# ScalarE instead of GpSimd forms the diagonal blocks for the convolution and the skip term

## The chip, the core and the metric

The kernel runs on one core of a Trainium2 chip. The core has five engines that run side by side and meet at semaphores: TensorE (PE in the rows, its weight loads PEld), VectorE (DVE), ScalarE (ACT), GpSimd (POOL) and SyncE (SP), which only issues DMAs here. The metric is the device time of one execution in microseconds (us), the median of several runs.

## What is computed

A small tower over 32 sequences of 257 tokens with 256 channels: a tokenizer, a layer of four Mamba blocks and a mixture of experts, and a layer of attention and a gated feed-forward part. The change touches only the Mamba blocks, which take the first 9,700 us. Cut to what matters:

```python
def _mamba_block(x, ...):                       # DI = 512 channels, N_ = 16 states, K_ = 4 taps
    xz = _layer_norm(x, g, b) @ in_w
    xs, z = jnp.split(xz, 2, axis=-1)
    xc = conv_general_dilated(xs, conv_w, ..., feature_group_count=DI)   # each channel by itself
    xc = silu(xc + conv_b)
    delta = softplus(xc @ xd_w @ dtp_w + dtp_b)
    dA  = exp(delta[..., None] * A)
    dBx = (delta * xc)[..., None] * Bm[:, :, None, :]
    y = _ssm_scan(dA, dBx, Cm) + D * xc                                  # D * xc is the skip term
    return y * silu(z) @ out_w + res
fwd = blk(blk(x, 0), 1);  bwd = blk(blk(x[:, ::-1], 2), 3)[:, ::-1]
```

## The kernel before

**Jobs.** The sequences are taken two at a time, in 16 groups; a group needs four Mamba blocks, so there are 64 jobs (one block on two sequences), one after the other. A job is of kind 0 to 4: kind 0 is the first of all, then a loop runs 15 times over kinds 1, 2, 3 and 4 (kind 4 is the first block of the next group), and the last group has kinds 1, 2 and 3 alone. That makes 1, 16, 16, 16 and 15 jobs of kinds 0 to 4. A last phase of some 1,700 us does everything behind the Mamba layer, and the change does not touch it.

**States and units.** Channels lie on the 128 partitions, in four chunks c. A job walks through 64 states s = 16 c + n. For each state ScalarE writes the decays exp(delta A) (`decays`, L714), GpSimd writes B times u (`b_times_u`, L489, called bu below), VectorE scans the two sequences with two instructions (`scan`, L912) and multiplies by C (`c_times_h`, L928), for every fourth state (s = 1, 5, 9, ...) GpSimd does that product (L498), and TensorE adds the product to y by four transposes (`add_state`, L1159). Two states make a unit u = s // 2, so a job has units 0 to 31. Ordinary decays are kept for two states ahead only, in PSUM; six of a job go to a buffer in SBUF (early_decay, states 22 to 24 and 50 to 52, or two to six states later in kinds 2 and 4), so that ScalarE can run a silu with its two table loads meanwhile. bu is kept for four states.

**Work between the states.** Each engine has its own hand-written list of what it does in which unit; the lists meet only at semaphores, and each engine takes its instructions strictly in order. Between the scans of a job the next one is prepared: norm (ScalarE `centred` L586 and L589, `inverse_deviation` L596 and L599, VectorE `normalize` L882), input product, convolution, silu, projections, and the softplus for delta. Of that softplus VectorE does two SCALAR_TENSOR_TENSOR instructions for each chunk (`step_size`, L891 and L896) and GpSimd the last sum (L469) and the product u (L475). For chunks 0 and 1 of the next job VectorE's pair stands in units 29 and 30 of kinds 0, 1 and 3, and in units 30 and 31 of kinds 2 and 4. Once a job VectorE forms the product cb of two SBUF tensors (`first_gains`, L939, unit 9), and three times it takes a finished chunk of y from TensorE (`output`, L948).

**The diagonal blocks.** TensorE does the convolution as four products with diagonal matrices, one for each tap, and the skip term as one. GpSimd forms them from the identity: `conv_weights` writes four blocks of 128x128 for a chunk into diag_store (L448, and three times L450), `skip_weights` one into skip_diag (L460). A job has 16 + 4 = 20 such instructions, 1,280 in all. On GpSimd they stand at states 21 and 25 (chunks 0 and 1), 38 and 40 (chunks 2 and 3; 40 and 42 in kinds 2 and 4), and at states 12, 28, 44 and 60 (skip), each behind the bu of that state. GpSimd's bu of a state waits only for the scan four states earlier, so GpSimd works ahead, until its own product with C (L498) has to wait for the scan of that state.

```python
if s % NST == 12 and not (last and s > 3 * NST):
    skip_weights(g, jj, s // NST + 1)
if s in (21, 25):
    conv_weights(g, jj + 1, (s - 21) // 4)
if s in (2 * conv_at(jj) + 10, 2 * conv_at(jj) + 12):
    conv_weights(g, jj + 1, 2 + (s - 2 * conv_at(jj) - 10) // 2)
```

## Time and profile before

| | us |
|---|---|
| median of 3 runs | 11426.39 (11422.36 to 11435.52) |
| the profiled execution | 11426.99 |
| its span, from first to last instruction | 11425.2 |
| first scan of the first job | 120.8 |
| last scan of the last job | 9702.5 |
| a job of kind 1, 2, 3, 4 (window from first scan to first scan, one job each) | 140.7, 148.6, 155.2, 156.4 |
| busy: VectorE, TensorE, GpSimd, ScalarE | 8852.6, 8675.4, 7499.2, 5872.3 |

A row of the timeline gives the start in us from the span's start, the time, engine, line, operation, what is written and read, and in brackets how long the engine had been idle and what ended that. A repeated row has a count (x3) and the time from the start of the first to the end of the last. The jobs repeat each other closely: the two-input instructions of VectorE in units 29 to 31 start within 0.02 us of the same place in all jobs of a kind, and the one that takes 1.51 us in the rows of kind 1 below takes 1.50 or 1.51 us in all 32 jobs of kinds 0, 1 and 3.

### The profile page before, as it was taken

Reading aid. Unit: us, or ns where it says so; the run is one execution under the profiler, and the core shown is the slowest. Engines: PE = TensorE matmul, PEld = TensorE weight load, DVE = VectorE, ACT = ScalarE, POOL = GpSimd, SP = SyncE. Lnnn points to the kernel's source line nnn. Section 1 sums busy time; section 2 is a strip of 40 time slices with the busy share of each in tenths; the row PEclk is TensorE's granted clock in tenths of the full one; section 3 lists DMA queues with packets and bytes.
Section 4 is the critical chain, followed back from the end, with each engine's and each line's share of the span. In section 5 each row is a group of like instructions: output and inputs, shape, how many; then the busy total and the mean of one; then the engine's idle time right before and its main releaser. Section 6 shows DMA issues by size and latency. Waiting matters only on the chain. (4 is left out here: it accounts for less than half of the span.)

```text
span 11425.2 us, 153089 instructions
## 1 busy us (share of the span) xinstructions
PE 8675.4 (76%) x42776; PEld 6977.0 (61%) x42776; DVE 8852.6 (77%) x13553; ACT 5872.3 (51%) x8819; POOL 7499.2 (66%) x7270
## 2 busy tenths in 40 slices
PE   6777776777777777777777777777777776799998
PEld 5656565655656565656555656565565665577776
DVE  5888888888888888888888888888888889233332
ACT  4555555555555555555555555555555554244443
POOL 5877777777777777777777878777777777000000
PEclk8888887888888888888888888888888887899999
DMA  2212122222222122222222212222222211000000
GB/s 81 80 65 70 64 80 75 80 70 77 74 75 73 63 70 75 80 75 80 70 78 75 73 52 80 75 80 75 75 74 73 80 67 46 25 10 10 11 11 10
DMA packets 366103, 730.02 MB, mean 64 GB/s; under 512 B 143670, under 2 KB 188890, under 8 KB 365274
## 3 DMA queue, kind: packets, MB, share of 16 engines
q1 hardware_dynamic: 361560, 717.54, 18.4%
q8 instruction: 341, 5.59, 0.2%
q14 instruction: 488, 4.00, 0.1%
q10 hardware_dynamic: 3714, 2.89, 0.1%
HBM read 699.27 MB, written 21.05 MB: 63 GB/s over the span
## 5 line engine op out<-in xcount | busy, mean ns | idle before, releaser
L489 POOL TENSOR_TENSOR bu<-b_all,u_buf 128x514 f32<-128x514 f32 x4096 | 4943.6, 1231 | 427.0 <-DVE h_ps L912 362.3
L912 DVE TENSOR_TENSOR_SCAN h_ps<-decay,bu 128x256 f32<-128x256 f32 x5468 | 3727.1, 738 | 498.9 <-ACT decay L714 298.4
L714 ACT ACTIVATE decay<-delta,neg_a 128x512 f32<-128x512 f32 x3712 | 2541.8, 688 | 3045.8 <-DVE h_ps L912 2041.7
L1159 PE MATMUL y_ps<-ident,ch 128*128 128x128 f32 x16384 | 2693.5, 313 | 901.5 <-DVE ch L928 460.2
L1159 PEld LDWEIGHTS y_ps<-ident,ch 128*128 128x128 f32 x16384 | 2216.4, 162 | 1419.3 <-DVE ch L928 673.5
L498 POOL TENSOR_TENSOR ch<-ch,c_all 128x512 f32<-128x512 f32 x1024 | 1427.8, 1394 | 1596.5 <-DVE ch L912 1596.1
L928 DVE TENSOR_TENSOR ch<-h_ps,c_all 128x512 f32<-128x512 f32 x3072 | 1979.2, 672 | 0.0
L912 DVE TENSOR_TENSOR_SCAN ch<-decay,bu 128x256 f32<-128x256 f32 x1956 | 1439.4, 736 | 40.7 <-ACT decay L714 36.4
L1044 PE MATMUL w_ps<-xn,in_w 128*128 128x257 f32 x4096 | 1111.8, 417 | 221.1 <-ACT xn L605 160.1
L1044 PEld LDWEIGHTS w_ps<-xn,in_w 128*128 128x128 f32 x4096 | 806.6, 209 | 408.1 <-issue 166.2
L1044 PE MATMUL w_ps<-xs_pad,diag_store 128*128 128x257 f32 x4096 | 983.1, 386 | 12.4 <-ACT xc L632 12.4
L1507 POOL TENSOR_TENSOR rstd_F<-h_F 128x514 f32<-128x514 f32 x16 | 17.5, 1096 | 1434.0 <-DMA h_F<-h_mid 1434.0
L1044 PEld LDWEIGHTS w_ps<-xs_pad,diag_store 128*128 128x128 f32 x4096 | 754.6, 193 | 118.4 <-ACT xc L632 25.4
L912 DVE TENSOR_TENSOR_SCAN h_ps<-early_decay,bu 128x256 f32<-128x256 f32 x676 | 774.3, 1201 | 48.6 <-DVE sz L948 42.6
L1044 PE MATMUL w_ps<-sz,out_w 128*128 128x257 f32 x2048 | 527.9, 403 | 292.2 <-DVE cen L871 180.8
L948 DVE TENSOR_TENSOR sz<-w_ps,sz 128x512 f32<-128x512 f32 x256 | 176.5, 689 | 618.0 <-PE w_ps L1171 618.0
L1044 PEld LDWEIGHTS w_ps<-sz,out_w 128*128 128x128 f32 x2048 | 391.0, 199 | 362.2 <-DVE cen L871 186.8
L1152 PE MATMUL y_ps<-skip_diag,xc 128*128 128x128 f32 x2048 | 362.1, 334 | 251.2 <-ACT y_t L691 251.2
L1152 PEld LDWEIGHTS y_ps<-skip_diag,xc 128*128 128x128 f32 x2048 | 339.7, 244 | 280.1 <-ACT y_t L691 259.7
L1044 PE MATMUL w_ps<-dtbc,dt_w 32*128 32x257 f32 x1024 | 433.0, 545 | 64.6 <-ACT rstd L658 62.1
L1044 PE MATMUL w_ps<-xc,xp_w 128*64 128x257 f32 x1024 | 301.6, 459 | 131.8 <-ACT xc L638 131.8
L1171 PE MATMUL w_ps<-ident,y_t 128*128 128x128 f32 x1024 | 187.1, 314 | 259.1 <-ACT y_t L691 259.1
(250 smaller groups left out, 11519.9 us busy)
## 6 DMA issues: line engine op xcount, KB each, us to landing
b_all<-bc_dram SPq DMA_DIRECT2D x512, 514.0 KB, 4.8
c_all<-bc_dram SPq DMA_DIRECT2D x512, 514.0 KB, 6.3
in_w<-in_L_attn_in_w SPq DMA_DIRECT2D x64, 1024.0 KB, 5.0
x_in<-in_x SPq DMA_DIRECT2D x128, 256.0 KB, 2.6
out_w<-in_L_attn_out_w SPq DMA_DIRECT2D x64, 512.0 KB, 3.9
...
```

The costliest lines, as they stand in the source:

```text
L489: pool.tensor_tensor(bu[:, s % NBU, :, :].rearrange("p b s -> p (b s)"), b_all[:, n // NU, n % NU, :, :].rearrange("p b s -> p (b s)"), u_ ...
L498: pool.tensor_tensor(h, h, c_all[:, n // NU, n % NU, :, 1:], ALU.mult).then_inc(pool_c_done, 1)
L714: func(decay_slot(jj, s).rearrange("p (b t) -> p b t", b=NB), delta[:, c, :, 1:S], ACT.Exp, scale=neg_a[:, k, c, n:n + 1]).then_inc(decays ...
L912: last = dve.tensor_tensor_scan(h[:, cols], decay_slot(jj, s)[:, cols], bu[:, s % NBU, b, 1:], bu[:, s % NBU, b, 0:1], ALU.mult, ALU.add)
L928: dve.tensor_tensor(ch[:, s % NPR, :].rearrange("p (b t) -> p b t", b=NB), h_ps[:, s % NU, :].rearrange("p (b t) -> p b t", b=NB), c_all[: ...
L948: dve.tensor_tensor(sz[:, c, :, 1:], banks(f"y{c}", g, jj).rearrange("p (b t) -> p b t", b=NB), sz[:, c, :, 1:], ALU.mult).then_inc(read_o ...
L1044: last = pe.matmul(w[0:rows, b, 0:S], lhs, rhs, start=(i == 0), stop=(i == len(terms(b)) - 1))
L1152: pe.matmul(y_ps[:, k, :], xc[:, jj % 2, c, b, 1 + half * P:1 + (half + 1) * P], skip_diag[:, :], start=(k == 0), stop=False, skip_group_c ...
L1159: last = pe.matmul(y_ps[:, k, :], ch[:, s % NPR, k * P:(k + 1) * P], ident[:, :], is_transpose=True, start=False, stop=(n == NST - 1 and k ...
L1171: last = pe.matmul(w[:, k * P:(k + 1) * P], y_t[:, k, :], ident[:, :], is_transpose=True, start=True, stop=True, skip_group_check=True)
L1507: pool.tensor_tensor(rstd[s][:, :, :], h[s][:, 0, :, :], h[s][:, 1, :, :], ALU.add).then_inc(h_summed[s], 1)
```

## The change

Both helpers move from GpSimd's list to ScalarE's. An ACTIVATE with the function Identity and the diagonal's weights as its scale takes the place of each GpSimd instruction, one for one. They wait for the same events as before. On ScalarE `conv_weights` stands in units 10 and 12 (chunks 0 and 1) and in the units conv_at + 5 and conv_at + 6 (chunks 2 and 3; these are units 19 and 20, or 20 and 21 in kinds 2 and 4), and `skip_weights` in units 5, 13, 21 and 29, each behind the unit's second ordinary decay. For the first job they stand in the preparation itself.

```diff
--- before.py
+++ after.py
@@ -433,33 +433,6 @@
             pool.affine_select(out=ident[:, :], in_=ident[:, :], compare_op=ALU.not_equal, fill=1.0, base=0,
                                pattern=[[-1, P]], channel_multiplier=1).then_inc(ident_set, 1)
 
-            def conv_weights(g, jj, c):
-
-                k = BLOCK_OF_JOB[jj % 4]
-                if c < 2:
-                    if positive(job_count(g, jj - 1, CI, CI)):
-
-                        pool.wait_ge(delta_ready, job_count(g, jj - 1, CI, CI))
-                else:
-                    pool.wait_ge(full_of(f"cv{c - 2}", g, jj), nth(f"cv{c - 2}", g, jj))
-                for tap in range(KW):
-                    weight = conv_w[:, k, c, tap:tap + 1]
-                    if tap == 0:
-                        last = pool.tensor_tensor(conv_diag[:, c % 2, tap, :], ident[:, :], weight.to_broadcast([P, P]), ALU.mult)
-                    else:
-                        last = pool.tensor_scalar(conv_diag[:, c % 2, tap, :], ident[:, :], weight, 1.0, ALU.mult, ALU.mult)
-                last.then_inc(diag_ready, 1)
-
-            def skip_weights(g, jj, c):
-
-                jj, c = jj + c // CI, c % CI
-                k = BLOCK_OF_JOB[jj % 4]
-                if positive(job_count(g, jj, STATES, NST * (c - 1) + 1)):
-
-                    pool.wait_ge(y_added, job_count(g, jj, STATES, NST * (c - 1) + 1))
-                pool.tensor_tensor(skip_diag[:, :], ident[:, :], d_skip[:, k, c:c + 1].to_broadcast([P, P]), ALU.mult
-                                   ).then_inc(skip_diag_ready, 1)
-
             def step_size(g, jj, c):
 
                 pool.wait_ge(sp_sums, job_count(g, jj, 2 * CI, 2 * c + 2))
@@ -518,9 +491,6 @@
             def lead_in():
                 pool.wait_ge(consts_loaded, 16 * n_const_dmas)
                 pool.wait_ge(ident_set, 2)
-                for c in range(CI):
-                    conv_weights(0, 0, c)
-                skip_weights(0, 0, 0)
                 step_size(0, 0, 0)
                 delta_x(0, 0, 0)
                 step_size(0, 0, 1)
@@ -536,16 +506,10 @@
                         step_size(g, jj, (s - 3) // 2)
                     if s % NST == 11 and s < 3 * NST:
                         delta_x(g, jj, s // NST + 1)
-                    if s % NST == 12 and not (last and s > 3 * NST):
-                        skip_weights(g, jj, s // NST + 1)
                     if s == 3 * NST + 6:
                         first_tokens(g, jj)
                     if last:
                         continue
-                    if s in (21, 25):
-                        conv_weights(g, jj + 1, (s - 21) // 4)
-                    if s in (2 * conv_at(jj) + 10, 2 * conv_at(jj) + 12):
-                        conv_weights(g, jj + 1, 2 + (s - 2 * conv_at(jj) - 10) // 2)
                     if s == STATES - 1:
                         step_size(g, jj + 1, 0)
                         delta_x(g, jj + 1, 0)
@@ -555,6 +519,29 @@
         @block.scalar
         def _(act):
             func = nc.scalar.activation
+
+            def conv_weights(g, jj, c):
+
+                k = BLOCK_OF_JOB[jj % 4]
+                if c < 2:
+                    if positive(job_count(g, jj - 1, CI, CI)):
+
+                        act.wait_ge(delta_ready, job_count(g, jj - 1, CI, CI))
+                else:
+                    act.wait_ge(full_of(f"cv{c - 2}", g, jj), nth(f"cv{c - 2}", g, jj))
+                for tap in range(KW):
+                    weight = conv_w[:, k, c, tap:tap + 1]
+                    last = func(conv_diag[:, c % 2, tap, :], ident[:, :], ACT.Identity, scale=weight)
+                last.then_inc(diag_ready, 1)
+
+            def skip_weights(g, jj, c):
+
+                jj, c = jj + c // CI, c % CI
+                k = BLOCK_OF_JOB[jj % 4]
+                if positive(job_count(g, jj, STATES, NST * (c - 1) + 1)):
+
+                    act.wait_ge(y_added, job_count(g, jj, STATES, NST * (c - 1) + 1))
+                func(skip_diag[:, :], ident[:, :], ACT.Identity, scale=d_skip[:, k, c:c + 1]).then_inc(skip_diag_ready, 1)
 
             def tokens(g, jj, c):
 
@@ -740,6 +727,7 @@
                 softplus_start(0, 0, 2)
                 softplus_powers(0, 0, 2)
                 act.wait_ge(setup_act, 7)
+                skip_weights(0, 0, 0)
                 for s in range(NDP):
                     decays(0, 0, s)
 
@@ -751,6 +739,8 @@
 
             def prepare_back(g, jj):
                 for c in (0, 2):
+                    conv_weights(g, jj, c)
+                    conv_weights(g, jj, c + 1)
                     conv_input(g, jj, c)
                     conv_input(g, jj, c + 1)
                     conv_output(g, jj, c)
@@ -847,6 +837,12 @@
                     lead(g, jj, NU * u + NDP, last)
                     after_even(g, jj, u, first, last)
                     lead(g, jj, NU * u + NDP + 1, last)
+                    if u % PAIRS == 5 and not (last and u > 3 * PAIRS):
+                        skip_weights(g, jj, u // PAIRS + 1)
+                    if not last and u in (10, 12):
+                        conv_weights(g, jj + 1, (u - 10) // 2)
+                    if not last and u in (conv_at(jj) + 5, conv_at(jj) + 6):
+                        conv_weights(g, jj + 1, u - conv_at(jj) - 3)
                     if u in silu_at(jj):
                         for i in range(NDS):
                             decays(g, jj, NU * u + NDP + 2 + i)
```

GpSimd, from the product with C of state 57 to that of state 61, in every job with a next one (before, then after; REGISTER_ALU computes a count to wait for):

```order
L498 TENSOR_TENSOR ch<-ch,c_all 128x512
L488 REGISTER_ALU
L489 TENSOR_TENSOR bu<-b_all,u_buf 128x514
L460 TENSOR_TENSOR skip_diag<-ident,d_skip 128x128
L489 TENSOR_TENSOR bu<-b_all,u_buf 128x514
L488 REGISTER_ALU
L489 TENSOR_TENSOR bu<-b_all,u_buf 128x514
L488 REGISTER_ALU
L489 TENSOR_TENSOR bu<-b_all,u_buf 128x514
L496 REGISTER_ALU
L498 TENSOR_TENSOR ch<-ch,c_all 128x512
```

```order
L471 TENSOR_TENSOR ch<-ch,c_all 128x512
L461 REGISTER_ALU
L462 TENSOR_TENSOR bu<-b_all,u_buf 128x514 x2
L461 REGISTER_ALU
L462 TENSOR_TENSOR bu<-b_all,u_buf 128x514
L461 REGISTER_ALU
L462 TENSOR_TENSOR bu<-b_all,u_buf 128x514
L469 REGISTER_ALU
L471 TENSOR_TENSOR ch<-ch,c_all 128x512
```

The skip block between the bu of state 60 and that of state 61 is gone, so the four bu follow each other directly.

ScalarE, units 12 and 13 of kind 4, around the silu of the gates (before, then after; sz is the gate, cen and sq belong to the norm of the next job):

```order
L714 ACTIVATE decay<-delta,neg_a 128x512
L714 ACTIVATE early_decay<-delta,neg_a 128x512 x3
L681 ACT_TABLE_LOAD
L681 ACTIVATE sz<-sz 128x2056
L682 ACT_TABLE_LOAD
L586 ACTIVATE sq<-w_ps 128x514
L589 ACTIVATE cen<-w_ps 128x514
```

```order
L701 ACTIVATE decay<-delta,neg_a 128x512
L534 ACTIVATE diag_store<-ident,conv_w 128x128 x4
L701 ACTIVATE early_decay<-delta,neg_a 128x512 x3
L668 ACT_TABLE_LOAD
L668 ACTIVATE sz<-sz 128x2056
L669 ACT_TABLE_LOAD
L544 ACTIVATE skip_diag<-ident,d_skip 128x128
L573 ACTIVATE sq<-w_ps 128x514
L576 ACTIVATE cen<-w_ps 128x514
```

Four blocks of the convolution now stand ahead of the three early decays and the silu, and one skip block between the silu and the norm. In the other kinds the silu of the gates stands in unit 9, ahead of all blocks of its surroundings.

## Rows read from the trace of the kernel before

**Rows 1.** Profile page: busy us by engine, then groups (count, busy, mean ns, idle)
```profile
PE 8675.4 (76%) x42776; PEld 6977.0 (61%) x42776; DVE 8852.6 (77%) x13553; ACT 5872.3 (51%) x8819; POOL 7499.2 (66%) x7270
...
L912 DVE TENSOR_TENSOR_SCAN h_ps<-decay,bu 128x256 f32<-128x256 f32 x5468 | 3727.1, 738 | 498.9 <-ACT decay L714 298.4
...
L948 DVE TENSOR_TENSOR sz<-w_ps,sz 128x512 f32<-128x512 f32 x256 | 176.5, 689 | 618.0 <-PE w_ps L1171 618.0
```

**Rows 2.** Groups of GpSimd by form, the same columns: the blocks
```profile
L450 POOL TENSOR_SCALAR diag_store<-ident,conv_w 128x128 f32<-128x128 f32 x768 | 273.0, 373 | 0.0
...
L448 POOL TENSOR_TENSOR diag_store<-ident,conv_w 128x128 f32<-128x128 f32 x256 | 121.4, 474 | 80.8 <-PE w_ps L1044 61.1 <-DMA ln_b<-in_L_attn_ln_b 19.7
L460 POOL TENSOR_TENSOR skip_diag<-ident,d_skip 128x128 f32<-128x128 f32 x256 | 102.3, 400 | 0.0
```

**Rows 3.** Timeline of ScalarE, start of the run: four of the new kind
```profile
24.96 1.26 ACT L728 ACTIVATE tok_ident<-ident,tok_wb 128x128 f32<-128x128 f32 x4
```

**Rows 4.** Timeline, GpSimd and VectorE, kind 1, unit 2
```profile
3287.90 1.26 POOL L469 TENSOR_TENSOR delta<-sp_l,rstd 128x514 f32<-128x514 f32 x1
...
3288.03 1.69 DVE L891 SCALAR_TENSOR_TENSOR sq<-sq 128x514 f32<-128x514 f32 x1
```

**Rows 5.** Timeline, GpSimd then VectorE, kind 2, units 29 and 30
```profile
3550.28 1.10 POOL L489 TENSOR_TENSOR bu<-b_all,u_buf 128x514 f32<-128x514 f32 x1
3551.33 0.41 POOL L460 TENSOR_TENSOR skip_diag<-ident,d_skip 128x128 f32<-128x128 f32 x1
...
3551.69 1.29 POOL L489 TENSOR_TENSOR bu<-b_all,u_buf 128x514 f32<-128x514 f32 x1
...
3552.93 1.10 POOL L489 TENSOR_TENSOR bu<-b_all,u_buf 128x514 f32<-128x514 f32 x1
...
3553.94 0.68 DVE L891 SCALAR_TENSOR_TENSOR diag_store<-diag_store 128x514 f32<-128x514 f32 x1
```

**Rows 6.** Timeline, GpSimd then VectorE, kind 1, units 29 and 30
```profile
3402.01 1.27 POOL L489 TENSOR_TENSOR bu<-b_all,u_buf 128x514 f32<-128x514 f32 x1
...
3404.76 1.26 POOL L489 TENSOR_TENSOR bu<-b_all,u_buf 128x514 f32<-128x514 f32 x1
...
3403.15 0.69 DVE L896 SCALAR_TENSOR_TENSOR sp_l<-sp_l,diag_store 128x514 f32<-128x514 f32 x1
...
3405.06 1.51 DVE L891 SCALAR_TENSOR_TENSOR sq<-sq 128x514 f32<-128x514 f32 x1
```

**Rows 7.** Timeline, ScalarE then VectorE, kind 1, units 10 to 13
```profile
3323.63 0.59 ACT L589 ACTIVATE cen<-w_ps 128x514 f32<-128x514 f32 x1
3326.73 0.69 ACT L596 ACTIVATE rstd<-w_ps,eps_t 128x514 f32<-128x514 f32 x1 [2.51 <-PE w_ps L1044]
...
3335.01 0.69 ACT L714 ACTIVATE decay<-delta,neg_a 128x512 f32<-128x512 f32 x1 [1.81 <-DVE h_ps L912]
...
3328.13 0.69 DVE L948 TENSOR_TENSOR sz<-w_ps,sz 128x512 f32<-128x512 f32 x1 [3.57 <-PE w_ps L1171]
```

**Rows 8.** Timeline of VectorE, kind 1, unit 9: cb
```profile
3314.09 0.41 DVE L939 TENSOR_TENSOR cb<-b_all,c_all 128x32 f32<-128x32 f32 x1
```

**Rows 9.** Timeline, ScalarE, TensorE, GpSimd, VectorE, kind 4, units 12 to 15
```profile
3774.90 1.94 ACT L714 ACTIVATE early_decay<-delta,neg_a 128x512 f32<-128x512 f32 x3
...
3788.56 0.60 PE L1171 MATMUL w_ps<-ident,y_t 128*128 128x128 f32 x4
...
3778.16 0.39 POOL L460 TENSOR_TENSOR skip_diag<-ident,d_skip 128x128 f32<-128x128 f32 x1
3778.52 3.55 POOL L489 TENSOR_TENSOR bu<-b_all,u_buf 128x514 f32<-128x514 f32 x3
...
3778.39 4.24 DVE L912 TENSOR_TENSOR_SCAN h_ps<-early_decay,bu 128x256 f32<-128x256 f32 x1 [0.40 <-POOL bu L489]
...
3789.79 0.68 DVE L948 TENSOR_TENSOR sz<-w_ps,sz 128x512 f32<-128x512 f32 x1
3790.69 2.20 DVE L882 TENSOR_TENSOR cen<-cen,rstd 128x514 f32<-128x514 f32 x2 [0.23 <-DVE sz L948]
```

## The prediction

> **What bounds the kernel now.** I read the page first, then the timeline of single jobs, unit by unit. VectorE is the busiest engine of the whole run, 8852.6 us, with TensorE close behind (8675.4); GpSimd has 7499.2 and ScalarE 5872.3 [rows 1]. All of VectorE's Mamba work lies ahead of 9702.5 us, and there it is the bound: its scans have only 498.9 us of idle time before them in 5468 instructions, and the largest single wait is that for a chunk of y from TensorE, 618.0 us before L948 [rows 1]. So I ask of each edit one question: does it move an instruction of VectorE, or something that VectorE waits for? Seconds taken from GpSimd are worth nothing in themselves.
>
> **What is removed.** GpSimd loses 768 instructions of 373 ns, 256 of 474 ns and 256 of 400 ns: 273.0 + 121.4 + 102.3 = 496.7 us [rows 2], 7.8 us a job. GpSimd works up to four states ahead and then waits for VectorE's scan at its own product with C, once in four states, so this time mostly becomes longer waiting there. Its direct worth is nil where a later bu still comes before its scan, which is everywhere but at two kinds of places costed below: where the change moves the moments at which the two engines meet in SBUF, and the stall of unit 12 of kind 4.
>
> **What is added.** ScalarE gets 1,280 instructions. The trace has none with a diagonal weight, but four of the same function, size and operand sort, 1.26 us for four in a row [rows 3], 0.31 us each: 1280 × 0.315 = 403 us, ScalarE's busy time from 5872 to some 6275 us (a shorter one, if the first of the four carries a fixed start, would give 370). It remains the least busy. What counts is whether a decay comes late. In kind 1 ScalarE idles 2.51 us before L596 in unit 10, where a block of four (1.26) goes in, and 1.81 us before the decay of unit 12, where the second goes in [rows 7]. The blocks for chunks 2 and 3 (units 19 to 21) and the single skip instruction of 0.31 us stand where decays are two states ahead of VectorE, that is more than one scan pair (2 × 0.7 us). I take 0 for kinds 0 to 3; the bounds are 0 and 0.3 us a job (one skip instruction exposed), 0 and +15 us in all. The added ACTIVATEs are Identity and change no table: no table load is added. The lead-in pays the skip instruction ahead of the first decays, +0.3 us once, and the conv blocks stand beside loads.
>
> **What moves: where VectorE and GpSimd meet.** This is the term I think decides. In the trace a VectorE instruction with two SBUF inputs that arrives while a GpSimd instruction is running does not take its usual time. L891 began at 3288.03, while L469 of GpSimd ran from 3287.90 to 3289.16: it took 1.69 us [rows 4]. Undisturbed it takes 0.68 [rows 5]. The rest of L469 was 1.13, so the price is the rest plus 0.56. A second case: bu63 of kind 1 ran from 3404.76 to 3406.02, L891 began at 3405.06 and took 1.51 = 0.96 + 0.55 [rows 6]. So I use: time = rest of the GpSimd instruction + 0.55 us, against 0.66 to 0.69 with none running. The skip block between bu60 and bu61 takes 0.36 to 0.41 us; without it bu61, bu62 and bu63 come 0.36 us earlier, because nothing else holds them, while VectorE's instructions of units 29 and 30 stay where they are.
>
> Kinds 2 and 4 (31 jobs). Now bu60 starts at 3550.28 and the skip block at 3551.33; bu61 (1.29) and bu62 (1.10, from 3552.93 to 3554.03) follow, and L891 starts at 3553.94, in the gap between bu62 and bu63, and takes 0.68 [rows 5]. After: bu61 at 3551.33, bu62 at 3552.57, bu63 at 3553.61 to 3554.88 (1.27, as the bu63 of [rows 6] has it at 1.26). L891 arrives at 3553.94 with 0.94 of bu63 still to go: 0.94 + 0.55 = 1.49 instead of 0.68, **+0.81 us**. A scan follows it on VectorE and nothing there has been waiting for another engine, so it is passed on: 31 × 0.81 = +25.1 us. Bounds: 0, if VectorE wins the meeting as it does now, and 1.29 − 0.16 (a bu63 that starts just before L891) or 1.1 us: 0 to +34.
>
> Kinds 0, 1 and 3 (32 jobs). Now L896 at 3403.15 takes 0.69 beside nothing (bu61 of 3402.01 ends at 3403.28, 0.13 later), and L891 at 3405.06 takes 1.51 [rows 6]. After: bu61 runs from 3401.65, bu62 (1.10, as in [rows 5]) from 3402.88 to 3403.98, so L896 takes 0.83 + 0.55 = 1.38, +0.69. bu63 then follows at 3404.4 at the latest (behind L896, or from 3403.94 on if it goes first) and ends by 3405.65, while L891 has moved to 3405.75 (3405.06 + 0.69): nothing runs, 0.66 instead of 1.51, −0.85. Together **−0.16 us**, 32 × −0.16 = −5.1 us. The nearest miss: if bu63 ended 0.1 us later, L891 would be caught by its tail (0.1 + 0.55 = 0.65), which costs the same. Bounds: −0.85 (L896 not caught) and +0.69 (L891 still caught): −27 to +22 us.
>
> The skip blocks of states 12, 28 and 44 move bu in the same way, but only one instruction of VectorE with two SBUF inputs is near: cb at 3314.09, 0.41 us, in unit 9 of kinds 1 to 3 [rows 8], which bu22 would now meet after the skip block of state 12 is gone from ahead of it: up to 0.7 us. Two units later VectorE waits 3.57 us for y from TensorE [rows 7], whose chain does not pass through cb. That cover hides it; without it 48 × 0.7 = 34 us would be due.
>
> **Kind 4, units 12 to 15** (15 jobs) is the one place where ScalarE's additions are not covered. There the block of four stands ahead of the three early decays at 3774.90 [rows 9], and the skip instruction behind the silu ahead of the norm: 1.26 + 0.31 = 1.57 us on the chain early decays, silu, y to TensorE (L1171, ends at 3789.16 now) and output at 3789.79. Before that VectorE stood in a scan of 4.24 us, which had waited 0.40 us for bu28 and then stood until GpSimd's row of three bu was over: 3778.39 to 3782.6 against 3778.52 + 3.55 = 3782.07 [rows 9]. Without the conv block of state 25 and the skip block of state 28 bu28 comes in time and the three bu end 0.4 to 1 us earlier, so VectorE is some 1 us early at unit 14 and y 1.5 us late, and the output moves to about 3790.75: +0.96. But the first of the two L882 already waits 0.23 for sz and both together take 2.20 us where two of 0.65 would be 1.3 [rows 9], so one of them meets a bu; 0.96 later it would not, −0.9. Sum **+0.1 us**, ×15 = +1.5. Bounds: −1 (all of the scan's gain kept) and +1.57 (the chain exposed in full): −15 to +24 us.
>
> The Trainium skill, "SBUF — State Buffer", section "Who interferes with whom", says that a VectorE instruction with two SBUF inputs contends with a GpSimd instruction that reads SBUF, and that the shared ports are an exclusive lock held for the whole instruction. [rows 4] and [rows 6] agree up to the extra 0.55 us, of which the page says nothing. The scan of [rows 9] does not: by a lock per instruction it should have ended one GpSimd instruction later, near 3779.1, and not after three more bu. That is why the rival of waiting until GpSimd is idle has a chance below.
>
> **The sum.** 0.3 (lead-in) + 25.1 − 5.1 + 0 (cb) + 1.5 (kind 4) = +21.8 us on the profiled execution of 11426.99, which lies 0.6 us above the median of 11426.39 and within its runs; I take the median: 11426.4 + 21.8 = 11448.2, rounded to **11449** for the small exposures of ScalarE that I put at nothing. Other moments of contact that I have not listed give the forecast its own band of 11438 to 11462.
>
> **Rivals.** (1) *A lighter GpSimd lets VectorE run free, faster.* If the shift of 0.36 us costs no new meeting in kinds 2 and 4 (bu63 held back by L891 as now, since [rows 5] show VectorE going first when both want in), kinds 0, 1 and 3 lose part of the 1.51 (−0.4 each, −13 us) and kind 4 keeps 0.6 of the scan's gain (−9 us): 11404. For it: 496.7 us less of contact on the side that disturbs VectorE. Against: bu63 would start 0.33 us ahead of L891, not at the same moment. (2) *ScalarE and waiting until idle, slower.* If VectorE, once caught, stands until GpSimd has no further instruction, as the scan of [rows 9] did for three, L896 of kinds 0, 1 and 3 is caught by bu62 and stands through bu63 too: 3403.15 to about 3405.9 instead of 3403.84, +2.0, less the 0.85 of L891: +1.2 × 32 = 38 us on top of 25: with kind 4 at +1 × 15 that gives 11426 + 25 + 38 + 15 = 11504; if only the chain of kind 4 is exposed in full (1.57 × 15 = 24, over the 21.8 without its 1.5) it is 11470. I put the case at 11480. It decides once GpSimd's next bu is issued before VectorE is served. (3) *Nothing passes on.* A gain or loss at unit 30 is taken up by the waits for y (618.0 us [rows 1], 3.57 in unit 11 [rows 7]), as these depend on TensorE, not VectorE: 11428. Against: the chain to y itself begins with scans of the same job. (4) *The change does not do what it says*: the ACTIVATE is far slower than [rows 3] or the blocks come late for TensorE's convolution, whose products stand one or two units behind; a block 0.2 us late would still be hidden there. 11440 to 11500.
>
> **How the numbers follow.** Forecast 0.50, faster rival 0.15, slower rival 0.17, nothing passes on 0.15, the last 0.03. The range reaches from the faster rival's upper half, 11408, to the middle of the slower, 11480; outside lie half of each rival, and the last. About 0.2%, or 23 us, is what a measurement of this kernel can tell from no change: 11403.5 to 11449.2. The forecast sits on the upper edge, so its 0.50 splits evenly: 0.25 within, 0.25 slower. Rival (1) at 11404 splits too, 0.09 faster and 0.06 within; (2) is slower, 0.17, (3) within, 0.15, (4) slower mostly. Faster 0.10, same 0.46, slower 0.44.
>
> **What would show it.** In the profile after: GpSimd's busy time near 7,000 us and ScalarE's near 6,270; L891 at unit 30 of kinds 2 and 4 at about 1.5 us and not 0.68; L891 at unit 30 of kinds 0, 1 and 3 at 0.66 and L896 there at 1.38; the wait before L948 in unit 11 of kind 1 about 0.7 shorter than 3.57; the 4.24 us scan of kind 4 shorter, its y later. I am wrong if L891 in kinds 2 and 4 keeps 0.68, if decays of kinds 1 to 3 begin to end VectorE's waits, or if jobs of kind 2 (148.6 us now by the table) grow by other than 0.8 us.

## The result and the profile after

| | before | changed |
|---|---|---|
| median | 11428.99 us (13 runs) | 11457.66 us (13 runs) |
| profiled execution | 11426.99 us | 11455.52 us |

The ratio is 1.0024, with a 95% interval of 1.0015 to 1.0032: the changed kernel is 0.24% slower, +29 us between the medians, where +22 us was forecast (11449, from a median of 11426.4 before). In the two profiled executions the last scan of the Mamba phase ends at 9702.5 and 9727.6 us, +25.1 us; the rest is in the phase behind it, which the change does not touch, and within what runs differ by.

The page of the changed kernel, first its line of busy times, then two groups (count, busy, mean ns, idle before and by what), which answer [rows 1]:

```profile
PE 8678.4 (76%) x42776; PEld 6964.1 (61%) x42776; DVE 8888.0 (78%) x13553; ACT 6241.6 (54%) x10099; POOL 7044.9 (62%) x5990
...
L908 DVE TENSOR_TENSOR_SCAN h_ps<-decay,bu 128x256 f32<-128x256 f32 x5468 | 3723.9, 737 | 520.2 <-ACT decay L701 327.5
...
L944 DVE TENSOR_TENSOR sz<-w_ps,sz 128x512 f32<-128x512 f32 x256 | 176.6, 690 | 598.9 <-PE w_ps L1167 598.9
```

And ScalarE's two new groups, by form (they stand where [rows 2] stood on GpSimd):

```profile
L534 ACT ACTIVATE diag_store<-ident,conv_w 128x128 f32<-128x128 f32 x1024 | 323.6, 389 | 0.0
...
L544 ACT ACTIVATE skip_diag<-ident,d_skip 128x128 f32<-128x128 f32 x256 | 99.3, 388 | 0.2
```

GpSimd is 454 us less busy, ScalarE 369 us more (one by itself lasts 0.39 us, in a row they overlap and four take 1.27), and VectorE, which has no instruction more or less, is 35 us busier. No engine's total tells where 25 us went. The start-to-start time of the jobs does (mean of all jobs of a kind with one behind it, first scan to first scan, worked out from the starts of the scans in both traces):

| kind | jobs | before | after | difference | all jobs |
|---|---|---|---|---|---|
| 0 | 1 | 139.4 | 138.9 | -0.5 | -0.5 |
| 1 | 16 | 141.1 | 141.1 | 0.0 | -0.5 |
| 2 | 16 | 147.8 | 148.8 | +0.9 | +15.0 |
| 3 | 15 | 155.6 | 154.7 | -0.9 | -13.2 |
| 4 | 15 | 157.2 | 158.9 | +1.7 | +26.2 |

The lead-in is 1.5 us shorter and the last job 0.4, which makes +25.1 in all. Kind 4 is the loser, not kind 2 as the prediction's largest term had it.

**Units 29 and 30.** Timeline of GpSimd and VectorE in the changed kernel, first kind 2, unit 30 (answers [rows 5]; the two bu are those of states 62 and 63), then kind 1, units 29 and 30 (answers [rows 6]; bu62 starts at 3407.83, bu63 at 3408.89):

```profile
3557.28 2.33 POOL L462 TENSOR_TENSOR bu<-b_all,u_buf 128x514 f32<-128x514 f32 x2
...
3558.66 1.50 DVE L887 SCALAR_TENSOR_TENSOR diag_store<-diag_store 128x514 f32<-128x514 f32 x1
```

```profile
3407.83 2.78 POOL L462 TENSOR_TENSOR bu<-b_all,u_buf 128x514 f32<-128x514 f32 x2
...
3408.89 1.72 POOL L462 TENSOR_TENSOR bu<-b_all,u_buf 128x514 f32<-128x514 f32 x1
...
3408.10 1.39 DVE L892 SCALAR_TENSOR_TENSOR sp_l<-sp_l,diag_store 128x514 f32<-128x514 f32 x1
...
3410.71 0.67 DVE L887 SCALAR_TENSOR_TENSOR sq<-sq 128x514 f32<-128x514 f32 x1
```

The forecast was 1.49 for the first, where 0.68 stood, and 1.38 and 0.66 for the two of kind 1. Measured: 1.50, 1.39, 0.67, within 0.02 us in each of the first 30 jobs. In kind 2 bu63 ends at 3557.28 + 2.33 = 3559.61, 0.95 us behind VectorE's arrival, and 0.95 + 0.55 = 1.50.

**The product cb and its cover**, kind 1 (answers [rows 7] and [rows 8]):

```profile
3318.39 1.10 DVE L935 TENSOR_TENSOR cb<-b_all,c_all 128x32 f32<-128x32 f32 x1
...
3332.91 0.69 DVE L944 TENSOR_TENSOR sz<-w_ps,sz 128x512 f32<-128x512 f32 x1 [3.37 <-PE w_ps L1167]
```

cb takes 1.10 instead of 0.41, as feared; unit 9 is 0.70 us longer in kinds 1 to 3, and unit 11 0.64 to 0.82 shorter in the mean. The cover held.

**Kind 4, units 12 to 15**, where before had [rows 9]: the changed kernel's ScalarE, VectorE and TensorE.

```profile
3779.85 1.27 ACT L534 ACTIVATE diag_store<-ident,conv_w 128x128 f32<-128x128 f32 x4
3781.02 1.93 ACT L701 ACTIVATE early_decay<-delta,neg_a 128x512 f32<-128x512 f32 x3
...
3787.49 0.40 ACT L544 ACTIVATE skip_diag<-ident,d_skip 128x128 f32<-128x128 f32 x1
...
3791.04 0.60 ACT L573 ACTIVATE sq<-w_ps 128x514 f32<-128x514 f32 x1 [2.17 <-PE w_ps L1040]
...
3792.01 1.30 ACT L701 ACTIVATE decay<-delta,neg_a 128x512 f32<-128x512 f32 x2
...
3783.02 3.02 DVE L908 TENSOR_TENSOR_SCAN h_ps<-early_decay,bu 128x256 f32<-128x256 f32 x2
3785.96 1.69 DVE L908 TENSOR_TENSOR_SCAN ch<-early_decay,bu 128x256 f32<-128x256 f32 x1
...
3792.74 1.40 DVE L908 TENSOR_TENSOR_SCAN h_ps<-decay,bu 128x256 f32<-128x256 f32 x2 [1.59 <-ACT decay L701]
...
3796.68 0.69 DVE L944 TENSOR_TENSOR sz<-w_ps,sz 128x512 f32<-128x512 f32 x1 [1.37 <-PE w_ps L1167]
3797.61 1.30 DVE L878 TENSOR_TENSOR cen<-cen,rstd 128x514 f32<-128x514 f32 x2 [0.23 <-DVE sz L944]
...
3788.92 1.23 PE L1040 MATMUL w_ps<-x_b,mean_w 128*128 128x257 f32 x2 [6.80 <-ACT cen L576]
...
3792.50 2.75 PE L1040 MATMUL w_ps<-sq,mean_w 128*128 128x257 f32 x8
...
3795.96 0.60 PE L1167 MATMUL w_ps<-ident,y_t 128*128 128x128 f32 x4
```

TensorE there in the kernel before:

```profile
3782.52 1.22 PE L1044 MATMUL w_ps<-x_b,mean_w 128*128 128x257 f32 x2 [5.04 <-ACT cen L589]
...
3785.95 1.90 PE L1044 MATMUL w_ps<-sq,mean_w 128*128 128x257 f32 x8
```

Counted from the first scan of unit 13 (3774.15 before, 3779.10 after), TensorE starts x_b at 8.37 and now at 9.82, +1.45: the chain of ScalarE, sized at 1.57. Then its eight products with sq take 2.75 where they took 1.90, and y is out of TensorE at 17.46 where it was at 15.01, +2.45. The two windows over those products, before and after, with busy time, granted clock, DMA share and GB/s:

```profile
3785.95:3787.85 1.90, 1.90 (x12) 1.00 0.00 0
```

```profile
3792.50:3795.20 2.70, 2.70 (x11) 0.68 0.00 0
```

The same products ran at full clock, 2.4 GHz, before, and for the larger part at 1.2 GHz now, after TensorE had idled 6.80 us instead of 5.04. This is no single case: they take 2.74 to 2.77 us in all 15 jobs of kind 4 now, and took 1.90 in 13 of 15 before (3.18 in the other two). VectorE was through the first three scan instructions on early decays 1.2 us sooner (3.02 for two and 1.69 for the third, where the first alone took 4.24), and spent it, and more, in two waits that were not there: 1.59 us before scan 31, whose decay stands on ScalarE behind the norm, and 1.37 before y.

**The loop's edge.** Behind kind 4 the loop goes back to kind 1. GpSimd's first bu of kind 1, before and after (the same edge in both):

```profile
3873.20 1.27 POOL L489 TENSOR_TENSOR bu<-b_all,u_buf 128x514 f32<-128x514 f32 x1 [3.78 <-issue]
```

```profile
3880.98 1.27 POOL L462 TENSOR_TENSOR bu<-b_all,u_buf 128x514 f32<-128x514 f32 x1 [3.51 <-issue]
```

GpSimd was ready and waited for nothing that the profile shows. Over the 15 changes from kind 4 to kind 1 the median of this wait is 3.91 us before and 3.23 after; at the end of the kinds 1, 2 and 3 it is 0.22. VectorE stands at the same place for that bu. Unit 30 of kind 4 became 0.84 us longer, and unit 31 0.71 shorter.

Fourteen of these changes go back to the loop's start. At the fifteenth the loop is left, and the same bu, the first of the two in this row of the kernel before, waits 0.13 us (a row shows idle times from 0.15 us on):

```profile
9288.49 2.78 POOL L489 TENSOR_TENSOR bu<-b_all,u_buf 128x514 f32<-128x514 f32 x2
```

SyncE issues the loads of B and C there within 0.1 us of the places that they have at the other changes, counted from the scan of state 62. So the long wait belongs to the way back to the loop's start, and not to the loads by themselves.

### The profile page after: what moved, and what is told of

It is laid out like the page before. It is cut to its first block and busy times, and to the rows that moved or that the text cites. A ratio compares the mean times of both kernels' runs of the same rounds, so it can differ in the third digit from the quotient of the medians.

```text
span 11453.7 us, 152968 instructions
## 1 busy us (share of the span) xinstructions
PE 8678.4 (76%) x42776; PEld 6964.1 (61%) x42776; DVE 8888.0 (78%) x13553; ACT 6241.6 (54%) x10099; POOL 7044.9 (62%) x5990
```

## Experiments

All ratios are to the kernel before, run on the same chip beside each experiment.

| run | what | median us | ratio (95%) |
|---|---|---|---|
| changed kernel | | 11457.7 | 1.0024 (1.0015 to 1.0032) |
| e1 | last skip block of a job back on GpSimd | 11477.6 | 1.0044 (1.0030 to 1.0058) |
| e2 | kind 4's blocks behind the norm | 11415.6 | 0.9987 (0.9978 to 0.9996) |
| e3 | only the skip blocks on ScalarE | 11417.8 | 0.9990 (0.9981 to 0.9999) |
| e4 | only the convolution's on ScalarE | 11464.2 | 1.0030 (1.0018 to 1.0041) |
| e6 | nothing formed behind the first job | 11414.0 | 0.9989 (0.9979 to 0.9998) |
| e7 | e1, GpSimd's loop 36 instructions further | 11460.2 | 1.0033 (1.0023 to 1.0043) |
| e5 | e2, meetings of units 29 and 30 avoided | 11402.8 | 0.9981 (0.9971 to 0.9990) |
| e9 | e5, those of units 2, 3 and 31 too | 11399.9 | 0.9971 (0.9961 to 0.9981) |
| e10 | before, VectorE held 0.6 us at unit 30 | 11447.0 | 1.0008 (0.9999 to 1.0018) |
| e11 | before, VectorE held 1.8 us at unit 30 | 11507.1 | 1.0063 (1.0046 to 1.0080) |

**e2: kind 4's blocks behind the norm**

```diff
+                    late = jj == 4 and u in (12, 13)
-                    if u % PAIRS == 5 and not (last and u > 3 * PAIRS):
+                    if u % PAIRS == 5 and not (last and u > 3 * PAIRS) and not late:
                         skip_weights(g, jj, u // PAIRS + 1)
-                    if not last and u in (10, 12):
+                    if not last and u in (10, 12) and not late:
                         conv_weights(g, jj + 1, (u - 10) // 2)
...
                     after_odd(g, jj, u, first, last)
+                    if jj == 4 and u == 15:
+                        skip_weights(g, jj, 2)
+                        conv_weights(g, jj + 1, 1)
```

> The changed kernel, but in kind 4 the four blocks of conv chunk 1 (unit 12) and the skip instruction of unit 13 stand behind the silu and the norm, at the end of unit 15. Theory A says that kind 4 has its own loss, which I had put at +0.1 us: in the traces its units 12 to 15 take 1.0 us more and unit 17 0.6 more than before. With the blocks behind, early decays and y0 come 1.57 us earlier: -1.0 x 15 - 0.6 x 15 = -24 us, 11434, and up to 8 us better still if the scan of unit 14 keeps its 1.0 us gain. Rival B (meetings at units 29 and 30 explain it all, unit 12 to 17 only shifts waits): within 5 us of the changed kernel's 11458.

Measured: 11415.6 against the changed kernel's 11457.7, 0.0037 less in the ratio, some 42 us, more than the 24 to 32 expected, and the sign turns: e2 is faster than before. In its trace kind 4 is 3.0 us a job shorter than in the changed kernel (2.1 in unit 15, 0.6 in unit 17, 0.3 in unit 26), 15 × 3.0 = 45 us. ScalarE and VectorE of e2 in kind 4, units 13 to 15:

```profile
3769.70 1.93 ACT L701 ACTIVATE early_decay<-delta,neg_a 128x512 f32<-128x512 f32 x3
...
3776.18 0.60 ACT L573 ACTIVATE sq<-w_ps 128x514 f32<-128x514 f32 x1
...
3786.07 1.26 ACT L534 ACTIVATE diag_store<-ident,conv_w 128x128 f32<-128x128 f32 x4
...
3781.14 1.40 DVE L912 TENSOR_TENSOR_SCAN h_ps<-decay,bu 128x256 f32<-128x256 f32 x2
...
3785.31 0.69 DVE L948 TENSOR_TENSOR sz<-w_ps,sz 128x512 f32<-128x512 f32 x1 [1.59 <-PE w_ps L1171]
```

The early decays come directly behind the ordinary one, scan 31 no longer waits, and of the two new waits only that for y is left. The 1.59 us of these rows are the exception: this is the one job of the 15 in which the products with sq ran slowly (2.97 us at 0.64); in the other 14 the wait is 0.40 to 0.43 us, against 1.37 in the changed kernel. Five instructions of 1.6 us on ScalarE, in one of five kinds of job, are thus the whole loss, and they cost 2.7 to 3 us each time. Rival B (they cost nothing) is out. Which part of the 42 us is ScalarE's delay and which the lower clock behind it, this run does not separate; both go with the five instructions.

**e3 and e4: each part alone**

e3 gives GpSimd back its conv_weights and the two calls of it, word for word as before, and takes those of ScalarE out; e4 does the same with skip_weights:

```diff
 e3, GpSimd
+                    if s in (21, 25):
+                        conv_weights(g, jj + 1, (s - 21) // 4)
+                    if s in (2 * conv_at(jj) + 10, 2 * conv_at(jj) + 12):
+                        conv_weights(g, jj + 1, 2 + (s - 2 * conv_at(jj) - 10) // 2)
 e3, ScalarE
-                    if not last and u in (10, 12):
-                        conv_weights(g, jj + 1, (u - 10) // 2)
-                    if not last and u in (conv_at(jj) + 5, conv_at(jj) + 6):
-                        conv_weights(g, jj + 1, u - conv_at(jj) - 3)
 e4, GpSimd
+                    if s % NST == 12 and not (last and s > 3 * NST):
+                        skip_weights(g, jj, s // NST + 1)
 e4, ScalarE
-                    if u % PAIRS == 5 and not (last and u > 3 * PAIRS):
-                        skip_weights(g, jj, u // PAIRS + 1)
```

> One part alone: only the skip blocks are formed on ScalarE, the convolution's stay on GpSimd where they were. Theory A: the STT of units 29 and 30 last as in the changed kernel (1.50 in kinds 2 and 4; 1.38 and 0.67 in the others), which is +25 - 5 us, of which the end of kind 4 absorbs 10: +10 us over before, and kind 4's y is 0.3 us later, +0 to +5: 11439 to 11444 against 11429 of before. Rival B (the cause is the convolution's blocks on ScalarE in kind 4): 11429 to 11432.

> The other part alone: only the convolution's blocks on ScalarE, the skip blocks on GpSimd. Theory A: units 29 and 30 as before; kind 4 has 1.26 of the 1.57 us on its chain: +1.2 x 15 = +18 us, and kinds 1 to 3 nothing: 11445 or so against 11429; together with the skip part alone it makes up the 28 us of the whole. Rival B (kind 4 explains all): 11455. Rival C (a GpSimd that is lighter by the convolution's 6 us a job is a gain of its own): below 11429.

The skip part alone is faster than before (0.9990), where I had expected +10 to +15 us; the convolution's part alone is as slow as the whole (1.0030). For e3 rival B was the nearer one, though neither had a gain in it. e4 is +34 us by its ratio (+21 to +47), above both theory A (+16) and rival B (+26), and only rival B lies in the interval. The trace of e3 is that of its fastest run, 15 us below its median, so its small differences are worth less than those of the others. In it VectorE's instructions of units 29 and 30 are as in the changed kernel (unit 29 of kinds 0, 1 and 3 0.69 longer, unit 30 of kinds 2 and 4 0.84 longer than before), so these meetings stand in a kernel that is no slower than before. Kind 4 is 1.2 us shorter than before in the mean, of which unit 14 has 0.36, a scan of 3.87 us for 4.24, unit 25 0.36 and unit 31 0.87.

The two runs also tell what the scan of 4.24 us of [rows 9] hung on. GpSimd and VectorE of e3 there (the four bu are those of states 28 to 31):

```profile
3766.78 4.60 POOL L479 TENSOR_TENSOR bu<-b_all,u_buf 128x514 f32<-128x514 f32 x4
...
3768.07 3.87 DVE L925 TENSOR_TENSOR_SCAN h_ps<-early_decay,bu 128x256 f32<-128x256 f32 x1 [0.41 <-POOL bu L479]
```

With the convolution's blocks on GpSimd and no skip block, VectorE still waits 0.41 us for bu28, and the scan still stands until 0.56 us behind the end of GpSimd's row (3766.78 + 4.60 = 3771.38), past three bu, in all 15 jobs. In e4, with the skip block and without the convolution's, VectorE does not wait for bu28, and the first four early scans take 0.76, 1.70, 1.51 and 1.11 us. So the long scan comes with the convolution's blocks, which make bu28 late, and not with the skip block. Why a scan that had to wait for its bu is not served between the next two stays open.

**e6: nothing formed**

```diff
-                for tap in range(KW):
+                for tap in range(1 if tiny else KW):
                     weight = conv_w[:, k, c, tap:tap + 1]
-                    last = func(conv_diag[:, c % 2, tap, :], ident[:, :], ACT.Identity, scale=weight)
+                    cols = slice(0, 1) if tiny else slice(0, P)
+                    last = func(conv_diag[:, c % 2, tap, cols], ident[:, cols], ACT.Identity, scale=weight)
...
+                cols = slice(0, 1) if tiny else slice(0, P)
-                func(skip_diag[:, :], ident[:, :], ACT.Identity, scale=d_skip[:, k, c:c + 1])
+                func(skip_diag[:, cols], ident[:, cols], ACT.Identity, scale=d_skip[:, k, c:c + 1])
```

(tiny is true for all calls but those of the first job.)

> The changed kernel, but behind the first job each block is written as one column only (128x1), by one ScalarE instruction for a block of four: neither GpSimd nor ScalarE carries the work, so the convolution and the skip term compute with blocks that are left from the first job. Theory A (the ScalarE load costs only in kind 4's units 12 to 17): kind 4's u12 to 17 as in run e2 or 0.3 us less, 11405 to 11418. Rival B (ScalarE's blocks also cost in kinds 1 to 3, where units 15 and 17 are 0.1 us longer each): 11395 or less. Rival C (kind 4's blocks on ScalarE cost nothing and e2's gain was something else): near the changed kernel's 11458.

11414.0, ratio 0.9989, the same as e2 (0.9987) and e3 (0.9990), as theory A had it. So the blocks that ScalarE forms outside kind 4's units 12 and 13 cost nothing that can be measured (each interval is some 10 us wide to either side), as the prediction took it. Taking the rest of the work off both engines brings no more than e2's placement, some 12 us below before. It is no bound for every placement: VectorE's instructions and the longer unit 30 are in e6 as in the changed kernel.

**e1 and e7: the last skip block back on GpSimd, and where the code lies**

```diff
 e1, GpSimd
+                    if s == 3 * NST + 12 and not last:
+                        last_skip_weights(g, jj, 4)
 e1, ScalarE
-                    if u % PAIRS == 5 and not (last and u > 3 * PAIRS):
+                    if u % PAIRS == 5 and u < 3 * PAIRS:
                         skip_weights(g, jj, u // PAIRS + 1)
 e7, GpSimd, ahead of the loop
                 pool.wait_ge(consts_loaded, 16 * n_const_dmas)
-                pool.wait_ge(ident_set, 2)
+                for _ in range(73):
+                    pool.wait_ge(ident_set, 2)
```

(last_skip_weights is before's skip_weights. The 73 waits become 36 more instructions.)

> The changed kernel with one of its 20 blocks a job given back: the skip block of state 60 is formed by GpSimd again, between bu60 and bu61; all else stays on ScalarE. Theory A (meetings of VectorE and GpSimd at units 29 and 30): the first STT of unit 30 takes 0.68 us again in kinds 2 and 4 (1.50 in the changed kernel), L892 of unit 29 0.69 and L887 of unit 30 1.51 in kinds 0, 1 and 3. By the durations alone that is -0.82 x 31 + 0.15 x 32 = -21 us, but at the end of kind 4 GpSimd waits some 3.3 us (3.9 before) for nothing that the profile shows ahead of the next job's first bu, which seems to absorb 0.7 of the 0.84 there: then -0.82 x 16 - 0.14 x 15 + 0.15 x 32 = -10 us, 11448 against the changed kernel's 11458. Rival B (the ScalarE chain of kind 4 is the whole cause): within 3 us of the changed kernel.

> The kernel of run e1 with 36 more instructions (waits that are long met) in GpSimd's program ahead of the loop; the loop itself and all timing inside are the same, but its code lies 36 instructions further, where that of before begins. In e1 GpSimd idles 5.39 us at the loop's edge (3.91 before, 3.23 in the changed kernel), ahead of kind 1's first bu, with its last instruction ready at the same place. Theory A (it waits for its own code, and how much has to be fetched depends on where the loop lies): the wait changes by 0.5 us or more, and the time by 15 times that. Rival B (it waits for something in the data, such as the loads of B): 5.3 to 5.5 us again, and the same time as e1, 11470 or so.

e1 should have given back 10 us and is 20 us slower than the changed kernel instead (ratio 1.0044 against 1.0024). Its durations did what was expected (0.68 at unit 30 of kind 2, units 29 and 30 of the other kinds as before), but GpSimd's wait at the loop's edge has a median of 5.39 us. e7, with the same loop and 36 instructions that do nothing ahead of it, has 3.77, and a median of 11460 for 11478. The waits differ at the 14 edges (4.6 to 6.5 us in e1, 3.6 to 5.4 in e7, but 11 of those 14 under 4.2), the times do not clear the noise: the intervals of the two ratios overlap, e1's five runs lie between 11456 and 11494, and the one that was profiled is the fastest of them, 11456.5, below the 11459.1 of e7's. The same bu of e1 and of e7 (an edge below e1's median):

```profile
3885.61 1.27 POOL L472 TENSOR_TENSOR bu<-b_all,u_buf 128x514 f32<-128x514 f32 x1 [4.62 <-issue]
```

```profile
3880.68 1.27 POOL L472 TENSOR_TENSOR bu<-b_all,u_buf 128x514 f32<-128x514 f32 x1 [3.79 <-issue]
```

So the wait depends on where GpSimd's loop lies in its program; that it waits for its own code is the reading that fits. The page lists two queues of the kind "instruction" that move 9.6 MB in the run, and of one of them (q14, packets of 8 KB) four packets start inside the wait at 13 of e1's 14 edges, three at all of e7's, two at 12 of the changed kernel's, and none where the loop is left. The profile does not say for which engine they are. The Trainium skill, "Runtime: NRT & Kernel Launch", section "Instruction fetch mechanics", says that a taken branch to code outside the fetched window forces a DMA fetch before execution goes on, and that code comes in 16 KiB blocks; the trace agrees that only the edge of the loop shows such a wait (medians of 3.1 to 5.4 us against 0.22 at other job changes, and 0.13 where the loop is left).

A second thing moves it. Two pairs of kernels have the same program on GpSimd and differ in VectorE's unit 30 of kind 4. In e10, further down, it is 0.59 us longer than before, and the wait is 3.50 and not 3.91; in e2 it is 0.84 longer than in e5, and the wait is 3.27 and not 3.74. So 0.4 to 0.5 of the 0.71 us of unit 31 go with VectorE's delay, and the rest would be left for GpSimd's new program. It is no rule: e11, with 1.79 us more in unit 30, has 3.50 like e10, and e9, whose unit 30 is 0.74 longer than e5's, has 4.04. That the loads of B and C, which start earlier with a longer unit 30, are less in the way of a fetch does not hold up either: the store ahead of them stands 16.9 us before the scan of state 62 in the kernel before, 17.8 in the changed one, and 17.7 in e9, whose wait is the longer. The reason stays open.

One more run, e8, put the same 36 instructions into the changed kernel:

> The changed kernel with 36 more such instructions ahead of GpSimd's loop. Theory A (code): the wait at the loop's edge, 3.23 us in the changed kernel, may change or not, as its place was a good one already; by rival B (data) it stays at 3.2 within 0.2.

There the wait stays (3.10 for 3.23), and the one time, 11461.2, is within what the changed kernel shows. A place of the code that was good stays good under this shift; it tells nothing more.

**e5 and e9: VectorE's two-input instructions moved out of GpSimd's row**

e5, VectorE, on top of e2 (size is the pair of step_size of a unit):

```diff
-                    if size:
+                    late = size is not None and u == 30
+                    early_c0 = size is not None and u == 29
+                    if size and not late:
                         step_size(*size, 0)
                     scan(g, jj, s + 1, 0)
                     if s + 1 in POOL_C:
                         c_times_h(g, jj, s)
+                        if late:
+                            if size[2] == 1:
+                                step_size(g, jj + 1, 0, 1)
+                            step_size(*size, 0)
                         scan(g, jj, s + 1, 1)
...
-                    if size:
+                    if size and not early_c0:
                         step_size(*size, 1)
```

> The kernel of run e2 (kind 4's blocks behind the norm), and VectorE's two-input instructions of units 29 and 30 moved out of GpSimd's row of bu60 to bu63: in kinds 0, 1 and 3 L892 of chunk 0 goes from unit 29 to unit 30, and L887 of unit 30 stands behind the product with C of state 60 instead of ahead of scan 61, in all kinds. Theory A (each meeting costs the rest of the bu + 0.55 us, and is passed on): 0.69 us less in 32 jobs and 0.82 less in 16 jobs of kind 2; in kind 4 the 0.82 is given back by GpSimd's wait at the loop's edge but for 0.14: -22 - 13 - 2 = -37 us against e2's 11416: 11379. Rival B (the meetings only shift waits for y and B): 11410 to 11420.

e9 replaces this with a list of what stands behind the product:

```diff
+                    behind = []
+                    if u == 2:
+                        behind = [(g, jj, 2, 0), (g, jj, 2, 1), (g, jj, 3, 0)]
+                    elif size and u == 30:
+                        n = g, jj + 1
+                        behind = [(*n, 0, 1), (*n, 1, 0)] if size[2] == 1 else [(*n, 0, 0), (*n, 0, 1), (*n, 1, 0)]
```

> Run e5 taken further: VectorE's two-input instructions of the step sizes stand in one row behind the product with C of state 4 (chunk 2, and the first one of chunk 3) and of state 60 (kinds 2 and 4: chunk 0 and the first one of chunk 1), where GpSimd is through with its row of bu and waits for the scan of state 5 or 61. In e5 they still meet GpSimd in unit 2 (0.35 us over their undisturbed time), unit 3 (1.01) and in kinds 2 and 4 in unit 31 (1.01). Theory A (each meeting is a loss that is passed on): 1.36 x 63 + 1.01 x 31 = 117 us less than e5's 11403: 11286. Theory C, formed from e5 and e7: only a part is passed on, the rest comes back as longer waits for TensorE, for B and at the loop's edge: e5 kept 7 to 13 of 37 us; by that share, 0.2 to 0.35, 23 to 41 us less: 11362 to 11380.

VectorE of e5 at unit 30 of kind 2, and of e9 in unit 2 of kind 1, where the three instructions stand in a row:

```profile
3540.88 0.68 DVE L891 SCALAR_TENSOR_TENSOR diag_store<-diag_store 128x514 f32<-128x514 f32 x1
```

```profile
3265.81 0.68 DVE L891 SCALAR_TENSOR_TENSOR diag_store<-diag_store 128x514 f32<-128x514 f32 x1
3266.53 0.69 DVE L896 SCALAR_TENSOR_TENSOR sp_l<-sp_l,diag_store 128x514 f32<-128x514 f32 x1
3267.14 0.69 DVE L891 SCALAR_TENSOR_TENSOR sq<-sq 128x514 f32<-128x514 f32 x1
```

The busy times of e9:

```profile
PE 8707.0 (76%) x42776; PEld 6989.9 (61%) x42776; DVE 8744.5 (77%) x13553; ACT 6241.6 (55%) x10099; POOL 6980.9 (61%) x5990
```

These meetings are gone (cb's stays), and VectorE is 8888.0 - 8744.5 = 143 us less busy than in the changed kernel. Of that e5 kept 7 us by the ratios (0.9981 against e2's 0.9987, 37 expected; the intervals overlap, so it may be nothing), and e9 11 more (0.9971, 117 expected by theory A). Both miss theory A. The traces tell where some of it went.

Part of it was never to be had. In kinds 2 and 4 of e9 unit 30 is 0.74 us longer than in e5, because it holds one instruction of unit 31 more, and unit 31 is only 0.12 shorter in kind 2 and not shorter in kind 4. VectorE comes to its end sooner and waits for GpSimd's first bu of the next job; GpSimd is ready for that bu 4.1 us behind the scan of state 62 in e5 and in e9. The first scan of the job behind kind 2 in e9, where e5 has no wait:

```profile
3544.52 1.40 DVE L912 TENSOR_TENSOR_SCAN h_ps<-decay,bu 128x256 f32<-128x256 f32 x2 [1.32 <-POOL bu L462]
```

This wait is 0 in e5 and 1.31 us in e9 in the mean of the jobs of kind 2, and 3.36 and 4.78 in those of kind 4. The meeting of unit 31 was hidden by GpSimd's own work, and the moved instruction costs 31 × 0.74 = 23 us in unit 30. In units 2 and 3, e9 is 1.27 us shorter than e5, and units 4 and 5 are 0.34 and 0.50 longer in kinds 1, 2 and 4.

Part of it went to TensorE's clock. The products with sq in kind 4 take 1.90 us at a granted clock of 1.00 in 14 of 15 jobs of e2, 2.24 at 0.85 in e5 and 2.70 at 0.70 in e9 (medians), each after 5.34 us of idle time. e9:

```profile
3764.70 1.22 PE L1052 MATMUL w_ps<-x_b,mean_w 128*128 128x257 f32 x2 [5.35 <-ACT cen L576]
...
3768.28 2.93 PE L1052 MATMUL w_ps<-sq,mean_w 128*128 128x257 f32 x8
```

Unit 15, where VectorE waits for the y behind them, is 0.20 us longer in e5 than in e2 and 0.47 longer again in e9 (medians). In e5 unit 30 of kind 2 is 0.84 shorter than in e2, and units 16, 17 and 26 of the same kind are 0.28, 0.37 and 0.50 longer in the median (all three wait for ScalarE or TensorE), and the loop's edge 0.48. The granted clock of TensorE in units 16 to 19 of kind 2 was 0.98 in e2 and 0.93 in e5 in the mean of its jobs. That the gain was lost to the clock alone isn't shown, nor why the clock is lower.

e9 is the fastest kernel of the study: 0.29% faster than before (0.19% to 0.39%), and 0.5% faster than the changed one.

**e10 and e11: the price of a delay at unit 30, by itself**

The kernel before with nothing moved, and one sum in e10, three in e11, behind L891 in unit 30 of kinds 2 and 4:

```diff
                         step_size(*size, 0)
+                    if u == 30 and jj in (2, 4) and not last:
+                        dve.tensor_reduce(cb[:, 0, 0:1], c_all[:, 7, 0, :, :].rearrange("p b s -> p (b s)"), AX.X, ALU.add)
                     scan(g, jj, s + 1, 0)
```

> The kernel before, with one more VectorE instruction at unit 30 of kinds 2 and 4 (the place at which the change makes L891 0.82 us longer): a sum over 514 elements of c_all into a cell of cb that nobody reads, about 0.6 us; GpSimd and ScalarE are as before. It measures alone what a delay of VectorE costs there. Theory A (passed on in full): 31 x 0.6 = +19 us. Theory C (kind 4's is taken up at GpSimd's loop edge, kind 2's partly by the waits for the output projection in unit 6 of kind 3): at most +0.3 x 16 + 0.1 x 15 = +6 us, which is hardly to be told from nothing, and in the traces unit 30 is 0.6 longer, GpSimd's wait at the edge 0.5 or so shorter and unit 6 of kind 3 0.3 shorter.

> Run e10 with three of the added sums at unit 30 of kinds 2 and 4 instead of one, 1.8 us a job, since e10's interval (-1 to +21 us) leaves open whether a delay of VectorE there is passed on. Theory A (in full, as the prediction's term of +25.1 us has it): 31 x 1.8 = +56 us over before. Theory C (kind 4's is taken up by GpSimd's wait at the loop's edge as far as that reaches, some 0.7 us, and kind 2's by waits of kind 3 for 0.3 to 0.4): 16 x 1.45 + 15 x 1.1 = +40 us. Theory D (waits take up most of it, whatever its size): below +25 us.

VectorE of e10:

```profile
3559.71 0.67 DVE L891 SCALAR_TENSOR_TENSOR diag_store<-diag_store 128x514 f32<-128x514 f32 x1
3560.30 0.67 DVE L988 TENSOR_REDUCE cb<-c_all 128x1 f32<-128x514 f32 x1
3560.89 0.74 DVE L912 TENSOR_TENSOR_SCAN ch<-decay,bu 128x256 f32<-128x256 f32 x1
```

Each sum holds VectorE 0.59 us. e10 came out at +9 us (-1 to +21), for 18 put in, which left all theories standing. e11 has +72 us (+53 to +91), for 31 × 1.79 = 55 put in: theory A, and perhaps more; theories C and D are out. In the total, a delay of VectorE at unit 30 is passed on. It is not passed on job by job: in e11's trace kinds 2 and 4 are 35 and 10 us longer in sum than before, where 29 and 27 were put in, and kinds 1 and 3, which have no added instruction, 16 and 19; why those grew stays open. I had formed C from e5 and e7, where removing such a delay brought little, and it was wrong for adding one.

## Why the prediction was right, and where only its sum was

- **Total.** 11449 forecast, 11458 measured, inside the range and inside the band of the forecast. The direction was right.
- **Units 29 and 30** (+25.1 and -5.1 us). The durations came out within 0.01 us, the rule "rest + 0.55" holds, and e11 shows that a delay there is passed on in the total. But the term was too large by what is taken back in unit 31 of kind 4, at the loop's edge, 0.71 of 0.84 us in 15 jobs, about 10 us (0.4 to 0.5 of it by VectorE's delay, as the pairs e10 and before, e2 and e5 show). I had read the 0.84 as passed on because nothing near it waited; that the next job's first scan waits for GpSimd at a wait that no record explains I had not priced.
- **Kind 4, units 12 to 15** (+0.1 us a job, +1.5 in all). This is the step that failed. The chain was sized right (1.57 against 1.45 measured), and so was the end of the collision of L882 (1.30 for two now, 2.20 before). What was wrong is that I set VectorE's gain at unit 14 off against the chain. VectorE waits for that chain; being early brings nothing. And the chain grew on TensorE: its products of the norm ran for the larger part at the low clock, +0.85 us in the job shown, a term that the prediction did not have. In the traces units 12 to 15 are 1.0 us longer and unit 17 0.6; against the same kernel with the blocks behind the norm (e2) the loss is 3 us a job, 45 in all. Against before, all that changed in kind 4 but units 30 and 31 is 1.6 us a job, 24 in all, just at the bound I gave; against e2 it is above.
- **ScalarE in kinds 0 to 3 at nothing.** Right: e2, e3 and e6 agree within 0.0003.
- **cb** at +0.7 us, hidden by unit 11: right.
- **GpSimd's relief at nil** was too pessimistic. Taken off the path of kind 4 (e2), or with no block formed at all (e6), the kernel is 0.11 to 0.13% faster than before, in spite of the longer unit 30. By the trace of e2 most of it is kind 4, 1.3 us a job shorter than before, with 1.2 in units 13 and 14, which was the lower bound of that term.
- **Lead-in** +0.3 us: it is 1.5 shorter in this pair, but 3.0 longer in e2's trace, whose lead-in is the same code, so it says nothing.
- **Rivals.** The faster one named the right engine, but of its conditions only one came true, and only in e2's placement (11415.6): kind 4 keeps the gain at the long scan. L891 of kinds 2 and 4 was caught in every kernel without the skip block of state 60, unless it was moved away. The slower one's part on kind 4, "the chain exposed in full", is what happened, without its other part: no L896 stood through two bu. In the changed kernel each of the first three early scans meets one bu after another, at 1.5 to 1.7 us each, and there the rule of the Trainium skill ("SBUF — State Buffer", "Who interferes with whom") of a lock for one instruction fits. For the scan of [rows 9] it does not, nor for that of e3, which took 3.87 us past three bu. The prediction was right that this scan would shorten without the convolution's block ahead of bu28.

So it was luck that the sum was near, because errors cancelled: kind 4, without its units 30 and 31, cost some 23 us more than forecast, while the loop's edge gave back 10 and the jobs of kind 3 became 13 us shorter where 2 were forecast. Why kind 3 did (its unit 6, waiting for decays, is 0.36 us shorter) stays open. So does a part of why removing the meetings returned so little (e5, e9) when adding a delay costs in full (e11): the traces show the wait for GpSimd at the job change and the lower clock, which are not the whole.
